# Graph network with two layers: a new order of work between the layers, and an end in which ScalarE and VectorE share the last normalisation

## The reference

```python
msg = h[edge_src] + relvectors[edge_rel]                  # layer 0
red = segment_sum(msg, edge_dst, num_segments=N)
x = layernorm(x + gru_cell(red, h=x, w_ih, w_hh, b_ih, b_hh))
deg = segment_sum(1, src); vals = rsqrt(deg)[src] * rsqrt(deg)[dst]      # layer 1, with self loops
out = segment_sum(vals[:, None] * (x @ W.T)[dst], src, num_segments=N)
x = layernorm(x + out)
```

## Time and profile before

| | us |
|---|---|
| median of 3 runs (lowest, highest) | 2237.19 (2235.58, 2240.35) |
| profiled execution: its time | 2237.45 |
| its span, first to last instruction | 2235.6 |
| mean granted TensorE clock | 0.965 |
| busy: PE / PEld / DVE / ACT / POOL | 1951.2 / 1479.8 / 1713.0 / 908.5 / 1616.4 |
| chain of waits, share of the span: PE / POOL / issue / DVE | 35% / 27% / 16% / 12% |

### The profile page before, as it was taken

One profiled execution on the slowest core, in us unless ns is written; L12 is line 12 of the kernel. 1 busy time (PEld: TensorE's weight loads), 2 busy tenths in 40 slices (PEclk: granted clock), 3 DMA queues, 4 the chain that ended last, 5 costly groups with the idle time before them and its releaser, 6 DMA issues.

```text
span 2235.6 us, 42553 instructions
## 1 busy us (share of the span) xinstructions
PE 1951.2 (87%) x9408; PEld 1479.8 (66%) x9408; DVE 1713.0 (77%) x3015; ACT 908.5 (41%) x3068; POOL 1616.4 (72%) x1763
## 2 busy tenths in 40 slices
PE   4799888799999989999976998888978988777996
PEld 3567666567777766777745876666766666565885
DVE  5499999899999968888856996677757777444676
ACT  1100000256666634444436984376716776000123
POOL 6777777777777776777644777777777777777772
PEclk8899999899999999999987999999999999999998
DMA  5355555444444456667644333333333333333335
GB/s 146 111 166 166 176 166 165 130 140 143 142 143 142 140 159 176 192 184 220 186 129 144 106 105 106 104 105 106 105 106 104 106 105 106 104 105 106 106 105 157
DMA packets 134019, 302.47 MB, mean 135 GB/s; under 512 B 31128, under 2 KB 67506, under 8 KB 133640
## 3 DMA queue, kind: packets, MB, share of 16 engines
q0 software_dynamic: 79872, 218.21, 34.0%
q10 hardware_dynamic: 43508, 71.27, 9.5%
q1 hardware_dynamic: 10420, 10.38, 1.5%
HBM read 267.74 MB, written 38.40 MB: 137 GB/s over the span
## 4 chain that ended last, share of the span: by engine, by line
PE 35%; POOL 27%; issue 16%; DVE 12%; DVEq 4%; DMA 4%; ACT 2%; ACTq 1%; SPq 0%; POOLq 0%
POOL rows L574 26%; PE ps L1704 20%; PE ps L1900 4%; DVE sums L879 2%; DMA rows<-gdram,ids 2%; PE ps L1902 2%; PE ps L1920 1%; PE ps L1890 1%; DVE sums L942 1%; PE ps L1768 1%; PE ps L1858 1%; PE ps L1850 1%; DVEq L799 1%; DVEq L784 1%; DVE onehot L777 1%
## 5 line engine op out<-in xcount | busy, mean ns | idle before, releaser
L1704 PE MATMUL ps<-rows,onehot 128*128 x5632 | 1352.1, 393 | 160.8 <-SPq L432 75.9
L1704 PEld LDWEIGHTS ps<-rows,onehot 128*128 128x128 f32 x5632 | 1063.3, 193 | 386.6 <-issue 213.0
L574 POOL DMA_INDIRECT rows<-gdram,ids x832 | 789.8, 949 | 287.3 <-issue 230.9
L574 POOL DMA_INDIRECT rows<-in_x_dram,ids x832 | 800.2, 962 | 268.9 <-issue 237.7
L862 DVE TENSOR_TENSOR sums<-sums,ps 128x256 f32 x400 | 167.1, 418 | 310.5 <-PE ps L1704 296.2
L833 DVE SCALAR_TENSOR_TENSOR onehot<-tkey,node_p,ps 128x512 f32<-128x512 f32 x403 | 297.9, 739 | 7.7 <-issue 4.4
L879 DVE TENSOR_TENSOR sums<-ps,sums 128x800 f16<-128x800 f32 (+1 forms) x156 | 215.4, 1413 | 1.2 <-issue 1.2
L777 DVE SCALAR_TENSOR_TENSOR onehot<-tkey,node_p,ps 128x1024 f32<-128x1024 f32 x152 | 193.1, 1270 | 2.2 <-DVE steps_i L756 1.0
L1453 ACT ACTIVATE wT<-wT,a 128x208 f16<-128x208 f16 x312 | 116.2, 454 | 186.9 <-DVE wT L771 173.8
L1398 ACT COPY sums<-ps 128x256 f32<-128x256 f32 x49 | 18.3, 373 | 343.1 <-PE ps L1760 343.1
L1453 ACT ACTIVATE onehot<-bias,a 128x208 f16<-128x208 f16 x312 | 116.1, 454 | 67.0 <-DVE bias L771 67.0
(11 more groups left out here) (286 smaller groups left out, 2035.4 us busy)
## 6 DMA issues: line engine op xcount, KB each, us to landing
xpd<-sums ACTq DMA_DIRECT2D x48, 384.0 KB, 3.4
sums<-xpd ACTq DMA_DIRECT2D x48, 384.0 KB
rows<-in_x_dram,ids POOLq DMA_INDIRECT x832, 2.8
rows<-gdram,ids POOLq DMA_INDIRECT x832, 2.7
xt<-in_x_dram ACTq DMA_DIRECT2D x96, 128.0 KB, 2.3
gdram<-in_x_dram ACTq DMA_DIRECT2D x5, 1250.0 KB
gdram<-sums ACTq DMA_DIRECT2D x48, 128.0 KB
out_dram<-sums SPq DMA_DIRECT2D x5, 896.0 KB
```

The lines of the kernel that those rows point to most:

```text
L574: pool.indirect_dma_start(rows[:, at:at + D], None, source, bass.IndirectOffsetOnAxis(ap=lists(n, p)[:, s * h + k:s * h + k + 1], axis=0)) ...
L1704: prod = M.matmul(ps[:, h, 0:width], onehot[:, u % U, k, :], rows[:, bass.ds(at + k * stride, width)], start=(k == 0), stop=(k == q - 1))
```

## The change

It has these edits, all in work from tile 44 of the first layer on:

- The inverse roots of tiles 46 to 48 are computed in one call at tile 48 instead of two calls; tile 48's moments get a place of their own (`moments_at`).
- ScalarE's order in tiles 44 to 48: the copy of the counts goes ahead of the gates' tanh, the copy of the sums ahead of centring and loads.
- VectorE doesn't wait for ScalarE's last tile any more before the second walk.
- In the permutation VectorE makes a batch's one-hots in the last step of three (of two in the last batches) instead of the first; TensorE's batches come two steps later, the last ones one step, the marks one step later.
- ScalarE scales the first batch before it loads its own rows (`own_later`).
- At the end ScalarE copies fewer tiles ahead of normalising tiles 32 to 43, and puts the last two copies between them. It normalises tiles 44, 46 and 48, VectorE 45 and 47. The last tile is stored as rows 0 to 95 and rows 96 to 105.

```diff
@@ -83,7 +83,7 @@
 BATCHES = (WIN - PERMUTE) // 2
 SPLIT_LAG = 5
 QUAD = SUB // CH * 4
-LAST_ROOTS = ((44, 2), (46, 2), (48, 1))
+LAST_ROOTS = ((44, 2), (46, 3))
 LAST_NODES = {44: (40,), 45: (41,), 46: (42,), 47: (43, 44), 48: (45,), 49: (46, 47, 48)}
 GUESS = 0x5f3759df
 MAGIC = 1.5 * 2.0 ** 23
@@ -230,7 +230,7 @@
         beside = again(end_a, end_b)
         xpl = beside(2, G3)
         nn, dy = beside(D), beside(D)
-        st, mv = beside(6), beside(U, 2)
+        st, mv = beside(6), beside(U + 1, 2)
         var4, half4, sq4, root4 = (beside(U) for _ in range(4))
         beside = again(begin_b, end_b)
         gate = beside(2, 2 * D)
@@ -374,6 +374,10 @@
 
             return perm0[2 if q == NB - 1 else q % 2]
 
+        def moments_at(t):
+
+            return U if t == NT - 1 else t % U
+
         def group_of(t):
 
             return t // U if t < LAST_ROOTS[0][0] else next(
@@ -477,8 +481,10 @@
                 put(a, tiles, P)
             sp.wait_ge(s_od, NT - ROOTS[-1])
             put(ROOTS[-1], NT - 1 - ROOTS[-1], P)
-            put(NT - 1, 1, LAST)
-            sp.wait_ge(s_ost, (len(PUTS) + 2) * 16)
+            for p, z in LAST_PARTS:
+                sp.dma_start(out[(NT - 1) * P + p:(NT - 1) * P + z, :], sums1[p:z, (NT - 1) * D:NT * D]
+                             ).then_inc(s_ost, 16)
+            sp.wait_ge(s_ost, (len(PUTS) + 3) * 16)
 
         @block.gpsimd
         def _(pool):
@@ -1039,7 +1045,7 @@
             def permute_in(g, first, bufs, every, per):
 
                 def task(i, u):
-                    if u % every == 0:
+                    if u % every == every - 1:
                         q = u // every
                         slot = bufs[q % 2]
                         at = i * per + (g * NB + first + q)
@@ -1311,14 +1317,13 @@
                 if t == NT - 2:
                     dve.wait_ge(s_sum_n, NT + 1)
                     dve.sem_inc(s_acc[1], U)
-                blend(t, t % 2, t % U)
+                blend(t, t % 2, moments_at(t))
                 for first, tiles in LAST_ROOTS:
                     if first + tiles - 1 == t:
                         node_roots(first, first % U, tiles)
             settle()
             step(V.memset(sums1[:, (NT - 1) * D:B * D], 0.0))
             dve.sem_inc(s_sums0, 1)
-            dve.wait_ge(s_x1, NT)
             dve.wait_ge(s_own[0], len(OWN_FIRST) * 16)
 
             for g in range(CH):
@@ -1351,7 +1356,7 @@
                     collect(t - U + 1, U)
             collect(NT - 1, 1)
             final_roots(ROOTS[-1], NT)
-            for t in range(ROOTS[-1], NT):
+            for t in range(ROOTS[-1] + 1, NT, 2):
                 part = sums1[:, t * D:(t + 1) * D]
                 V.tensor_scalar(part, part, rs_all[:, t:t + 1], mean_all[:, t:t + 1], ALU.mult,
                                 ALU.add).then_inc(s_od, 1)
@@ -1494,7 +1499,7 @@
                 if not isinstance(t, int) or t >= U:
                     act.wait_ge(s_x1, t - (U - 1))
                     act.wait_ge(s_gev, t - (U - 2))
-                A.activation(yc[:, m, :], dy, ACT.Identity, bias=mv[:, m, 0:1], scale=-1.0).then_inc(s_yc, 1)
+                A.activation(yc[:, m, :], dy, ACT.Identity, bias=mv[:, moments_at(t), 0:1], scale=-1.0).then_inc(s_yc, 1)
 
             def put_g(t, m, group, rws):
 
@@ -1565,36 +1570,40 @@
             for t in range(J - WIN, NT):
                 first, *more = LAST_NODES[t]
                 tanh_of(t, t % 2)
+                if t < NT - 2:
+                    counts_over(t + 2)
                 if t < NT - 1:
                     open_gates(t + 1, (t + 1) % 2)
-                if t < NT - 2:
-                    counts_over(t + 2)
                 put_g(first, first % U, group_of(first), P)
                 for d in more:
                     put_g(d, d % U, group_of(d), P)
+                if t < NT - 2:
+                    sums_over(t + 2)
                 centre(t, t % U)
                 if t < NT - 2:
                     load_node(t + 2, t % 2, P if t < NT - 3 else LAST)
                 if t < NT - 3:
                     bring(t + 3, (t + 1) % 2)
-                if t < NT - 2:
-                    sums_over(t + 2)
             for d in LAST_NODES[NT]:
                 put_g(d, d % U, group_of(d), P if d < NT - 1 else LAST)
 
-            act.wait_ge(s_x1, NT)
-            act.wait_ge(s_sums0, 2)
-            for k in range(2):
-                act.wait_ge(s_gst[k], (NT + 1 - k) // 2 * 16)
-            for t in range(OWN_A, NT - 1, FG):
-                own_rows(t, min(FG, NT - 1 - t), 0, P, s_own[1])
-            for p, z in LAST_PARTS:
-                own_rows(NT - 1, 1, p, z, s_own[1])
+            def own_later():
+
+                act.wait_ge(s_x1, NT)
+                act.wait_ge(s_sums0, 2)
+                for k in range(2):
+                    act.wait_ge(s_gst[k], (NT + 1 - k) // 2 * 16)
+                for t in range(OWN_A, NT - 1, FG):
+                    own_rows(t, min(FG, NT - 1 - t), 0, P, s_own[1])
+                for p, z in LAST_PARTS:
+                    own_rows(NT - 1, 1, p, z, s_own[1])
 
             for g in range(1, CH):
                 for i in range(NB // 2):
                     for p in range(2):
                         values(i * 2 + (g * NB + p), perm1[p])
+                        if g == 1 and i == 0 and p == 0:
+                            own_later()
 
             def sums_turned(t):
 
@@ -1605,17 +1614,22 @@
 
             turned = 0
             for q, (a, z) in enumerate(zip((0,) + ROOTS, ROOTS)):
-                while turned < min(z + 5, NT):
+                while turned < min(z + (5 if q < 2 else 3), NT):
                     sums_turned(turned)
                     turned += 1
                 act.wait_ge(s_shift, q + 1)
                 for t in range(a, z):
-                    if (t - a) % 4 == 3 and turned < NT:
+                    if (t - a) % 4 == (3 if q < 2 else 1) and t - a > 1 and turned < NT:
                         sums_turned(turned)
                         turned += 1
                     part = sums1[:, t * D:(t + 1) * D]
                     A.activation(part, part, ACT.Identity, bias=mean_all[:, t:t + 1],
                                  scale=rs_all[:, t:t + 1]).then_inc(s_o, 1)
+            act.wait_ge(s_shift, len(ROOTS) + 1)
+            for t in range(ROOTS[-1], NT, 2):
+                part = sums1[:, t * D:(t + 1) * D]
+                A.activation(part, part, ACT.Identity, bias=mean_all[:, t:t + 1],
+                             scale=rs_all[:, t:t + 1]).then_inc(s_od, 1)
 
         @block.tensor
         def _(pe):
@@ -1983,13 +1997,13 @@
 
                 def earlier(i, u):
                     k = i * 3 * U + u
-                    if k > 3 and k % 3 == 1:
-                        joint_batch(ahead + k // 3 - 1, perm1[(k // 3 - 1) % 2])
+                    if k > 5 and k % 3 == 0:
+                        joint_batch(ahead + k // 3 - 2, perm1[k // 3 % 2])
 
                 def rest(i, u):
-                    if u in (1, 3, 5):
-                        joint_batch(ahead + THIRDS * U + u // 2 - 1, perm1[(u // 2 + 1) % 2])
-                    if u == 6:
+                    if u % 2 == 0:
+                        joint_batch(ahead + THIRDS * U + u // 2 - 2, perm1[u // 2 % 2])
+                    if u == 7:
                         marks(g + 1)
 
                 begin_chunk(g + 1)
```

## The result

| | before | after |
|---|---|---|
| median of 4 runs each (lowest, highest) | 2238.77 (2235.58, 2241.30) | 2219.82 (2217.95, 2222.39) |
| profiled execution: its time, its span | 2237.45, 2235.6 | 2219.05, 2217.2 |
| mean granted TensorE clock | 0.965 | 0.972 |

The changed kernel takes 0.9925 of the time of the kernel before, 95% interval 0.9912 to 0.9937: about 17 us faster (the medians in the table lie 18.95 us apart). The profiled execution is 18.4 us shorter.

What follows compares the result with a forecast made beforehand. GpSimd's second-layer gathers, unstopped from 1207.60, were taken to set the end, so their late start decides. 13.3 us up to group 14 plus 4.0 at the end make 17.3 off 2237.45: 2220.1 us, range 2215.8 to 2228.0.

Steps and rivals of the forecast that it cites:

- The frame: Second layer: from 1207.60 GpSimd's gathers run without a stop, and the end lies at a fixed distance behind them.
- Part 1: ScalarE's order in the last five first-layer tiles: counts and sums copies moved ahead, 3.2 us saved.
- Part 2: VectorE's roots of tiles 46 to 48 in one call: 2.6 us saved, memset ending 5.8 us earlier at about 1173.7.
- Part 3: VectorE at the second walk's start: step 3's one-hot at 1174.1 instead of 1184.04, batch 0's one-hots 1176.1 to 1179.1.
- Part 4: ScalarE's own-row loads behind batch 0's scaling: issues 8.72 + 1.6 us, gather group 14 at 1209.3 instead of 1222.64.
- The term: Gain up to the start of gather group 14: 13.3 us, 16.7 at the better bound.
- Part 5: The kernel's end, last normalisations and the split last store: 4.0 us gained, bounds 3.0 and 4.7.
- (a): Whole change: all goes at the better bound, 16.7 + 4.3 us gained, time 2216.4; chance 0.17.
- (b): Own-row load holds ScalarE 17.3 us, everything behind 7.0 us later, gain 6.3 + 4.0, time 2227.1; chance 0.20.
- (c): Between early gathers and end, TensorE rather than GpSimd sets the pace; only the tail's gain left, 2233.4; chance 0.06.
- (d): TensorE stays at its lower clock through the first batches, 7.3 us a group, so the kernel gets slower; chance 0.04.

Runs made afterwards that it cites:

- hots_first: The changed kernel with the batches' one-hots back in the first step of three and TensorE's batches and marks where they were before; 2225.28 us.
- one_store: The changed kernel with the last tile's 106 rows stored in one transfer; 2227.53 us in one run, last roots to end 8.04 us against 5.91.
- own_split: The changed kernel with three own-row loads behind batch 0's scaling, four behind batch 1's; 0.9924 of the kernel before on a slow chip, 2215.07 us (0.9909) on another.
- tensor_held: The changed kernel with 24 extra matmuls on TensorE, product unread, at the start of the third chunk's walk; 2220.35 us.
- own_split_early: own_split with VectorE making step 3's one-hot at tile 47, ahead of tile 48's gates; 2218.22 us, 0.9901 of the kernel before.

## Why the prediction was right, point by point

**The frame** held: GpSimd's gathers set the end once they run without a stop. Group 14 started 15.24 us earlier, and 14.8 of that are there at the last roots; the two kernels with extra work show both halves of it. Forecast 2220.1, measured 2219.82 in the median and 2219.05 in the profiled execution. TensorE waits behind 1215 for gathered rows more than for anything else (73.8 us in 53 waits, by SPq L436), which fits GpSimd as the bound.

**Part 1** (3.2 us): 3.06 at the gates of tile 48, and 3.0 counted from the gates of tile 47. The copy of the sums ran at 1158.84 against 1158.3, the inputs' matmuls at 1159.27 against 1158.7. One piece was not as priced: the 0.55 us in tiles 46 and 47 were lost, as TensorE's narrow inputs matmuls took 1.54 and 1.81 us for tiles 46 and 47 where they took 1.03 and 1.35: the granted clock in them was 0.64 and 0.51 and had been 1.00 and 0.77, with idle times of 4.67 and 3.65 us ahead of the two tiles' work where it had been 1.5 to 2.0 at a time. Its wide ones for tile 48 gave that back, 3.31 for 3.78.

**Part 2** (2.6 us, memset ending about 1173.7): it started at 1173.53, 5.5 us earlier where 5.8 were forecast. From the gates of tile 48 to the memset it is 9.68 us instead of 12.12, so 2.4 us. Three tiles cost a little more than one or two: one of the small instructions takes 0.38 us (L899 at 1171.14) where it took 0.15 and 0.17.

**Part 3** was the weakest step. The one-hot of step 3 came at 1174.98 (1174.1 said), and "two steps take 2.0 us when TensorE's results are there" failed: from 1174.98 to 1178.67 they took 3.7. The results were there, but VectorE idled 0.97 us behind the memset and 0.86 and 0.67 ahead of the two sums. The chain of waits fills these gaps with L834, VectorE's queue reading the words that say which columns and which sums a step uses: 0.30 us or more for a read and 0.19 for the arithmetic behind it. In the first three steps of a piece of the walk (a call of `walk_second`, L829) the code reads two words a step, in the later ones one. In the kernel before, the first steps' reads ran while VectorE was busy with batch 0's one-hots; with those moved behind, nothing covers them. hots_first shows it from the other side: the one-hots stand in front again, and the first sum has no idle time. Batch 0's one-hots ran at 1178.67, 2.6 us later than forecast. I had carried over a duration of two steps from a place where the reads were covered.

**Part 4** made up for it with an error of the other sign. The issues took 9.67 us where 10.3 were forecast, between the row's 8.72 and the bound of 17.3. But I had put them behind all of batch 0's scalings, and their first 4.1 us (1183.43 to 1187.57) ran beside the scalings. Batch 1's scaling therefore started at 1193.14, 2.4 us before the forecast's 1195.5. With batch 1 at 2.95, the lower clock's price, as I took it, group 14 started at 1207.40 against 1209.3. The term was 13.3 and measured 15.24: 1.9 too small. Batch 0's one-hots were 2.6 us late; from them to batch 1's scaling took 14.5 us where 19.4 were forecast, 4.9 less; from there to group 14 0.5 more. So the closeness of the total is luck in part: two errors of 2.6 and 4.9 us stand against each other in it.

**Part 5** (4.0 us): 3.6. Splitting the store was priced by the two engines in the row at 0.13 busy, and one_store confirms it with 2.1 us. The rest was priced as a store that drains ahead of the last ones, and the rows fit that, as told under one_store. The forecast weighed two sections of the Trainium skill, page "DMA: Bandwidth & Descriptors": "Rules for kernel authors", by which splitting a transfer into disjoint partition halves gives nothing, and "Why a DMA increments its semaphore by 16 and not by 1", by which 106 rows get two engines. For this row count the second decides: 1.6 us of last wait against 5.0.

**The rivals.** (a), all at the better bound, 2216.4: batch 1 ran at the lower level of the clock, so no. (b), the own-row load taking the place of the old wait: the mechanism was there, in small; it is what own_split removes, and it was worth 3.9 us of what was left. (c) fell by GpSimd's waits and by the distance from group 14 to the last roots; tensor_held agrees at the one place that it tests. (d), TensorE staying at its lower level: it was at it for most of steps 3 and 4 (granted clock 0.65), for batch 1 (0.50) and part of steps 10 to 12 (0.83), never for long. own_split_early shows the same mechanism eating a whole step's gain.

**The sum.** 17.3 forecast, 18.4 measured: 15.24 (13.3), -0.46 (0) and 3.62 (4.0).

## What to carry to other kernels

Where one engine runs like a conveyor behind a start that others delay, measure everything at the moment its last stop ends: gains ahead of that count whole, those behind it on other engines hardly at all. What ends a stop is the chain of the one group that waits, so moving a batch that has to wait behind another step helps as much as shortening the wait, and step counts decide which. Work that is moved away from the front of a loop can uncover what ran beside it: here VectorE's reads of step words. A store of an awkward number of rows at the very end is worth a look at the DMA share in the last microseconds.

## What the runs showed of the hardware that I had not expected

- ScalarE's DMA issues don't wait for activations that stand ahead of them in program order. In the changed kernel the first issue began at 1183.43 with eleven scalings still to come, in own_split_b the second part began 1.58 us into batch 1's scaling. The activations already handed over went on, and the next one behind the issues came at 1193.14, straight behind the last issue. The page "Perfetto Trace Analysis" of the Trainium skill, section "Sequencer Loop", has the sequencer push engine instructions into a queue and carry out control instructions itself. The rows agree if a DMA issue counts among the second, which that section doesn't say. That makes the issues' place between activations cheaper than it looks, by up to the queued work, 4.1 us here.
- Four of the seven own-row loads are 896 KB each, the others 128, 96 and 10. The first three issues took 0.38, 0.59 and 0.58 us in the changed kernel and the fourth 3.32. In own_split_b the fourth came 4.9 us behind the third and took 0.37, the fifth 2.17, and all seven 4.93 us instead of 9.67: the same loads cost ScalarE's queue half as much when spread.
- Reading a step's word into a register takes VectorE's queue time of its own: 0.30 us in most cases, up to 0.86 here, and 0.19 behind it. It shows only where VectorE has no other work beside it: 0.97 us behind the memset, then 0.86 and 0.67 ahead of two sums whose inputs were there. With the wait put back it was 1.90 ahead of the first sum, with step 3's one-hot moved away 1.94, in hots_first 0.79 behind the memset and none ahead of the first sum; the chain of waits has the queue's L834 in the gaps each time. The timeline puts the gaps ahead of the sums down to "issue", which says only that no other engine was waited for.
- Batches of TensorE behind idle times of 4.2 to 10.7 us took nearly twice their time (2.95 against 1.57 us), and two steps behind 5.4 to 11.4 us took 5.6 to 6.1 instead of 3.72; those behind idle times of 0.83 to 1.72 us took the usual one. In own_split_early sixteen matmuls behind 0.92 us of idle took the long one too (granted clock 0.61). What stood ahead of them was one step between two gaps.
